# Softmax attention layer: TensorE's order over two positions, with three maxima in a row and one unit beside the values

## The reference, cut to what matters

```python
x = x + _layernorm(_L0_attn_ref(_layernorm(x), W_qkv, b_qkv, W_proj, b_proj))
# inside _L0_attn_ref
qkv = x @ W_qkv + b_qkv                       # split into q, k, v; 16 heads of 16
att = einsum('bhqd,bhkd->bhqk', q, k) * SCALE
att = where(causal, att, -inf); att = softmax(att, axis=-1)
y = einsum('bhqk,bhkd->bhqd', att, v)
return y.reshape(B, T, C) @ W_proj + b_proj
x = x + _layernorm(_L0_ffn_ref(_layernorm(x), weight, disha))     # same stage of the kernel
```

## Time and profile before

| what | value |
|---|---|
| median of 3 runs | 4210.25 us (4207.5 to 4215.37) |
| the profiled execution's own time | 4209.16 us |
| its span, first to last instruction | 4207.4 us |
| mean granted TensorE clock | 0.965 |
| softmax stage, first score matmul of batch 0 to the first of batch 7 | 103.6 to 1179.6 us |

### The profile page before, as it was taken

One profiled execution on the slowest core, in us unless ns is written; L12 is line 12 of the kernel. 1 busy time (PEld: TensorE's weight loads), 2 busy tenths in 40 slices (PEclk: granted clock), 3 DMA queues, 4 the chain that ended last, 5 costly groups with the idle time before them and its releaser, 6 DMA issues. The chain is left out here.

```text
span 4207.4 us, 74610 instructions
## 1 busy us (share of the span) xinstructions
PE 3893.2 (93%) x28676; PEld 3028.3 (72%) x28676; DVE 2712.3 (64%) x7778; ACT 2115.5 (50%) x3994; POOL 1172.9 (28%) x1083
## 2 busy tenths in 40 slices
PE   4999999999999899999999999999999599999993
PEld 2444444444545788888888888888888499999992
DVE  5888888888785565555565565555555555555555
ACT  1566666666666555554455554554454333333333
POOL 3233343343333211111112111111111133333335
PEclk8899999999988999999999999999999799999996
DMA  3543544443441100000000000000001133333345
GB/s 70 99 97 57 97 92 67 87 98 61 77 110 43 36 26 21 22 21 21 20 22 22 22 19 19 16 20 10 20 20 34 52 65 65 73 69 65 65 122 173
DMA packets 177203, 230.73 MB, mean 55 GB/s; under 512 B 27388, under 2 KB 152411, under 8 KB 176848
## 3 DMA queue, kind: packets, MB, share of 16 engines
q1 hardware_dynamic: 148816, 189.53, 19.6%
q0 software_dynamic: 25728, 28.03, 4.5%
q10 hardware_dynamic: 2304, 8.39, 0.5%
HBM read 94.30 MB, written 87.05 MB: 43 GB/s over the span
## 5 line engine op out<-in xcount | busy, mean ns | idle before, releaser
L880 ACT ACTIVATE probs<-a_scores 128x1024 f32<-128x1024 f32 (+3 forms) x768 | 615.7, 811 | 337.7 <-PE a_scores L774 331.8
L1034 DVE CUSTOM_DVE_ANT_0 a_scores<-a_scores,mask 128x384 f32<-128x384 f32 (+3 forms) x1024 | 480.6, 514 | 101.9 <-PE a_scores L760 96.2
L774 PEld LDWEIGHTS a_scores<-q_st,k_st 50*128 50x128 f32 x1536 | 149.1, 191 | 355.4 <-issue 201.5
L273 POOL TENSOR_TENSOR l_ln_rstd<-l_ln_ve,minus_half 128x4 f32<-128x4 f32 x80 | 82.0, 1025 | 1047.5 <-DVE l_ln_ve L246 1047.1
L1842 ACT ACTIVATE l_o<-l_num,l_den 128x64 f32<-128x64 f32 x960 | 222.0, 319 | 292.6 <-DVE l_den L2328 281.1
L774 PE MATMUL a_scores<-q_st,k_st 50*128 50x512 f32 (+3 forms) x1536 | 349.9, 453 | 10.3 <-DVE mx L1034 4.0
L760 PE MATMUL a_scores<-k_st,q_st 48*128 48x512 f32 (+3 forms) x1536 | 305.9, 396 | 50.7 <-ACT probs L880 22.1
L1037 DVE TENSOR_REDUCE mx<-a_scores 128x2 f32<-128x1024 f32 x256 | 309.9, 1221 | 60.8 <-PE a_scores L760 60.1
L794 PE MATMUL a_out<-probs,v_aug 128*32 128x512 f32 (+3 forms) x3072 | 345.1, 523 | 3.4 <-POOL probs L961 3.2
L961 POOL TENSOR_SCALAR_AFFINE_SELECT probs<-probs 128x512 f32<-128x512 f32 x256 | 164.8, 645 | 518.5 <-ACT probs L880 507.3
L2664 PE MATMUL e_out<-e_weights_hi,e_hT_hi 128*128 128x256 f32 x1088 | 303.8, 279 | 0.0
(11 more groups left out here) (294 smaller groups left out, 10569.4 us busy)
## 6 DMA issues: line engine op xcount, KB each, us to landing
q_st<-parts SPq DMA_DIRECT2D x192, 128.0 KB, 4.5
k_st<-parts SPq DMA_DIRECT2D x192, 128.0 KB, 6.8
expert_rows_scratch<-empty_row SPq DMA_DIRECT2D x34, 520.0 KB, 9.5
l_x<-x_scratch SPq DMA_DIRECT2D x32, 512.0 KB, 3.8
e_weights<-in_L_ffn_W_dram SPq DMA_DIRECT2D x16, 1024.0 KB, 7.3
e_rows<-expert_rows_scratch SPq DMA_DIRECT2D x24, 390.0 KB
e_rows<-expert_rows_scratch SPq DMA_DIRECT2D x16, 520.0 KB
x_in<-in_L_attn_x_dram SPq DMA_DIRECT2D x8, 1024.0 KB, 5.5
```

Of the source, the lines that this page charges most:

```text
L774: last = nc.tensor.matmul(psum_r[:, R.slot(u), h2, 0:w], k_st[rows, 2 * hg + pair, i * P:(i + 1) * P], q_st[rows, 2 * hg + pair, q0:q0 + w ...
L880: nc.scalar.activation(probs[:, k % 3, 2 * pair:2 * pair + 2, 0:w], psum_r[:, R.slot(u), :, 0:w], ACT.Exp).then_inc(R.evacuated[R.slot(u)], 1)
L1034: last = nc.vector.tensor_tensor_reduce(s, s, mask[:, HALF - w:HALF], 1.0, LEAST, ALU.add, ALU.max, out[:, h2, :])
```

## The change

TensorE takes positions in twos, k even. The order before, over two positions (S scores, M maxima, V values, U unit; the position, then the pair; L is k+16):

`S k,0 | M L,0 | V k-2 | S k,1 | M L,1 | U k | S k+1,0 | M L+1,0 | V k-1 | S k+1,1 | M L+1,1 | U k+1`

The order after:

`S k,0 | M L,0 | S k,1 | V k-2 | M L,1 | M L+1,0 | M L+1,1 | U k | V k-1 | S k+1,0 | S k+1,1 | U k+1`

`r_units` numbers the ring in that order. On VectorE, at odd positions, the reduction of pair 0 comes before the taking out of the unit, where it came after it. ScalarE's and GpSimd's orders stay. No instruction is added or taken away, and none changes its size.

```diff
     def r_units(u0, with_head):
         units = {}
-        for k in range(NK):
-            for pair in range(2):
-                units["S", k, pair] = u0 + len(units)
-                if k + LM < NK or with_head:
-                    units["M", k + LM, pair] = u0 + len(units)
+        for k in range(0, NK, 2):
+            more = k + LM < NK or with_head
+            units["S", k, 0] = u0 + len(units)
+            if more:
+                units["M", k + LM, 0] = u0 + len(units)
+            units["S", k, 1] = u0 + len(units)
+            if more:
+                units["M", k + LM, 1] = u0 + len(units)
+                units["M", k + 1 + LM, 0] = u0 + len(units)
+                units["M", k + 1 + LM, 1] = u0 + len(units)
+            units["S", k + 1, 0] = u0 + len(units)
+            units["S", k + 1, 1] = u0 + len(units)
         return units
...
         def turn(b, U, RU, with_head, with_tail, prepare=None):
-            for k in range(NK):
-                more = k + LM < NK or with_head
+            for k in range(0, NK, 2):
+                more, of = k + LM < NK or with_head, b + (k + LM) // NK
                 scores(b, RU, k, 0)
                 if more:
-                    maxima(b + (k + LM) // NK, b, RU, k + LM, 0)
+                    maxima(of, b, RU, k + LM, 0)
+                scores(b, RU, k, 1)
                 if k > 1:
                     values(b, RU, k - 2)
                 elif with_tail:
-                    values(b - 1, RU_TURN, NK - 2 + k)
-                scores(b, RU, k, 1)
+                    values(b - 1, RU_TURN, NK - 2)
                 if more:
-                    maxima(b + (k + LM) // NK, b, RU, k + LM, 1)
+                    maxima(of, b, RU, k + LM, 1)
+                    maxima(of, b, RU, k + 1 + LM, 0)
+                    maxima(of, b, RU, k + 1 + LM, 1)
                 if k in UNIT_AT and kept(UNIT_AT[k], with_head, with_tail):
                     unit(batch_of(b, UNIT_AT[k]), b, U, UNIT_AT[k])
+                if k > 1:
+                    values(b, RU, k - 1)
+                elif with_tail:
+                    values(b - 1, RU_TURN, NK - 1)
+                scores(b, RU, k + 1, 0)
+                scores(b, RU, k + 1, 1)
+                if k + 1 in UNIT_AT and kept(UNIT_AT[k + 1], with_head, with_tail):
+                    unit(batch_of(b, UNIT_AT[k + 1]), b, U, UNIT_AT[k + 1])
...
                 what = UNIT_AT.get(k - 1)
+                if k % 2 == 1 and more:
+                    reduce(b, b, RU, mk, 0)
                 if what and what[0] in ON_DVE and kept(what, with_head, with_tail):
                     of = (b - 1 if what[0] in TAIL_UNITS else
                           b + 1 if what[0] in HEAD_UNITS or what == ("N", 4) else b)
                     take(of, b, U, what)
-                if more:
+                if k % 2 == 0 and more:
                     reduce(b, b, RU, mk, 0)
```

## The result

The changed kernel takes 4327.05 us (median of 4 runs, 4323.68 to 4335.19) against 4208.88 of the kernel before on the same chip: ratio 1.0285, 95% interval 1.0271 to 1.030. The forecast was 4228, range 4170 to 4290. The sign was right and the size was not: 118 us slower instead of 18.

What follows compares the result with a forecast made beforehand. VectorE's chain of reductions (143.6 us a batch), plus 6.7 where TensorE binds, gave 150.3; waits made it 156.0 against 153.4. Over the whole kernel +18 on 4209.2 gave 4227, median 4228 us, range 4170 to 4290.

Steps and rivals of the forecast that it cites:

- the three waits on top: Per softmax batch, beyond 150.3: bank for units +2.8, ScalarE's bursts +2.6, late VectorE at k = 4 and 8 +0.3.
- ACT in bursts: ScalarE: four exps arrive close together, layer-norm applications between some, so exps and second maxima come late; +2.6 us a batch.
- Chain and PE alone: Softmax batch: VectorE's chain 143.6 us, plus 6.7 where TensorE's own time is longer, makes 150.3.
- the one bank: VectorE takes out an even position's unit behind two reductions, so the next unit on TensorE waits; +2.8 us a batch.
- number u waits for u-3: Ring rule: position k+2's pair 0 scores wait for the reduction of the third maxima in a row.
- The chain of three reductions: VectorE has three reductions before the next two positions may start; its chain alone takes 143.6 us a batch.
- DVE's idle time: Sign of being right: VectorE's idle time in a batch rises from 20.8 us to 23 or more, before L1034 and L1037.
- PE's busy time would fall by 5 or more: Sign of being right: TensorE's busy time per batch down by 5 us or more, with more idle before L774.
- The unit beside the values: TensorE, unit next to values on all 128 rows: saves 0.15 us per two positions, bounds 0 and 0.30.
- The merged group: TensorE: score pairs in three groups instead of four save about 0.15; a middle 512-column pair costs about 0.25 us.
- Rival 4: ScalarE and VectorE starve in turn, at k = 12 to 18 and 24 to 27: +54, 4280 us; chance 0.20.

Runs made afterwards that it cites:

- the fill: Changed kernel with matmuls repeated while TensorE would wait: in positions 0, 1, 12, 13, 4309.31 us; also in 14 to 17 and 44 to 47, 4303.13 us.
- the two kernels with short reductions: Every VectorE reduction reads only the first 64 columns of its maxima, without the mask: kernel before 4171.27 us, changed kernel 4202.54 us.
- the alternating order: Kernel before with TensorE in twos, score groups of three, scores and maxima alternating, VectorE's order as in the change: 4328.15 us; with ScalarE's order fitted too, 4289.58 us.

## Why the prediction was right and wrong

- **The step that failed: the three waits on top, put at +5.7 a batch, above all "ACT in bursts" at +2.6.** Chain and PE alone were to give 150.3. At full clock the batch takes 165.6 with the fill, some 164.5 without (estimate: less about 1), so what stands on top of them is about 14, not 5.7, if the 150.3 is right. That is some 8.5 of the 12.9 us by which a batch missed (168.9 against 156.0). The part on the one bank was about right (38 and 39: by the prediction's prices 5.3 for PE and 1.0 for the bank, 6.33 measured). What was too small is the waiting of the maxima for slots that ScalarE holds: 25.1 us a batch, where it was 9.9. The sum took PE's times for the long units without the ring's waits in front of them. Positions 36 and 37 show it: by the prediction's prices they come to 6.88, 7.72 measured, at clock 1.00.

```profile
907.22 0.64 PE L801 MATMUL a_out<-probs,v_aug 128*32 128x256 f32 x8
907.99 1.36 PE L767 MATMUL a_scores<-k_st,q_st 48*128 48x512 f32 x6
908.38 0.18 PEld L767 LDWEIGHTS a_scores<-k_st,q_st 48*128 48x128 f32 x2 [0.20 <-DVE mx L1054]
908.91 0.19 PEld L767 LDWEIGHTS a_scores<-k_st,q_st 48*128 48x128 f32 x2 [0.34 <-ACT probs L897]
909.28 1.99 PE L699 MATMUL a_general<-w_ffn,yT 128*128 128x256 f32 x8
911.21 0.42 PE L801 MATMUL a_out<-probs,v_aug 128*32 128x128 f32 x8
911.56 0.62 PE L781 MATMUL a_scores<-q_st,k_st 50*128 50x384 f32 x4
```

  The three maxima take 1.29 from their issue to that of the unit (907.99 to 909.28), where 0.8 was counted. By the ring's numbers the second of them waits for the first maxima's reduction and the third for the exp of the second scores, and the two rows of weight loads (908.38, 908.91) show just these: two waits that the prediction's list never had, as it went from "number u waits for u-3" straight to the longest one. In this pair bound by PE they add in full, 0.5; 0.2 more is the first exp's slot (maxima at 1.67, where PE's own times give 1.47), and 0.15 the saving at the unit that wasn't there.
- **The clock: a term that the sum did not have.** The prediction read 1.00 in the batch of before and took it as given. A change that makes PE wait in long pieces doesn't keep that: two falls in a batch, 1.7 and 2.2 us by the fill, are some 4 of the missed 12.9 us a batch, and the clock brought back was worth 24 of the 100 us in all. The prediction had even named 12 and 13 among its longest pairs. It also never priced a matmul at the low level, though the run of before holds such stretches (0.97 over batches 0 to 6).
- **The chain of three reductions: right where it binds, and sized within 0.25.** Positions 0 and 1: 6.0 forecast, 6.17 measured; second maxima at 1.62, measured 1.68. Positions 12 and 13: 7.8, measured 8.03. DVE's idle time was to rise to 23 or more; it is 36.6. The third maxima moved away gave 0.7 back in such a pair at full clock, and about half of the loss over 18 pairs. The sign that PE's busy time would fall by 5 or more didn't come: it rose from 145.6 to 151.7.
- **The unit beside the values mostly saves nothing: the 0.15 taken for it was wrong, its bound 0 was right.** In the rows above the F unit costs 1.93 in front of the values, as against 1.92 in front of scores, and the values behind it 0.35, as before. This is what the rule in the Trainium skill, TensorEngine Tiling (Array Packing), Tiling Modes, says of 128x128 and 128x32 as two modes: the trace agrees, and by that rule the prediction's sum would have been some 10 us higher. The exception agrees with it too: unit N runs on 128x32 like the values, and from its start to the scores behind the values 1.19 pass (810.21 to 811.40), where N and the values of 512 columns took 0.34 and 1.00 apart (N from 739.70 to 740.04 in batch 4 before). The merged group does save: the middle one of S M S costs 0.24 (906.65 to 906.89), forecast 0.25.

```profile
906.65 0.40 PE L767 MATMUL a_scores<-k_st,q_st 48*128 48x512 f32 x2
906.89 0.40 PE L781 MATMUL a_scores<-q_st,k_st 50*128 50x512 f32 x2
...
810.21 0.30 PE L740 MATMUL a_general<-ident,mx 128*32 128x128 f32 x1
810.22 0.63 PE L801 MATMUL a_out<-probs,v_aug 128*32 128x512 f32 x3
...
811.40 0.44 PE L781 MATMUL a_scores<-q_st,k_st 50*128 50x384 f32 x2
```

- **Rival 4 (ACT and DVE starve in turn, 4280) was the nearest**, and had 0.20. Of its two places, 12 to 18 grew and 24 to 27 did not (12.86 against 12.77). It too left the clock out; with two falls a batch it would have given some 4310 (estimate). The range's upper end was built from this rival alone, and so missed by 37 us.

The sign of the change was forecast for a reason that holds for most of the loss, the reductions; the size was not. What stays open: the 31 us between the two kernels with short reductions, and with it how much of the waits is ScalarE's. The rows point to its four exps in a burst and to slots given back late; no run made its work shorter in this order. And where exactly the clock falls after a wait wasn't settled: the fill in one place moved it to the next.

## What to carry to other kernels

A ring of few slots ties its two readers together: before the writer's order is changed, write down for every slot whom it now waits for, not only for the one that looks longest, and turn the queues of both readers with it (in the alternating order ScalarE's unturned queue alone cost 39 us). An engine that showed waits of 10% spread thin may carry them at no price, and pay for the same waits when they stand in one piece, as TensorE's granted clock can fall behind them. Compare variants position by position at equal clock first; the total mixes the waits with what the clock does behind them.

## What the runs showed of the hardware that had not been expected

- The granted clock of TensorE fell to about 0.6 over positions 2, 3 and 14, 15 behind pairs in which PE was busy 5.2 of 6.2 and 5.1 of 8.0 us; the values of 512 columns there took 1.87 (786.25 to 788.12) instead of 1.00, as the timeline of PE after shows. With 16 more matmuls in the waits of 12 and 13, positions 14 and 15 ran at 1.00.

```profile
786.25 1.93 PE L801 MATMUL a_out<-probs,v_aug 128*32 128x512 f32 x8
788.12 0.90 PE L767 MATMUL a_scores<-k_st,q_st 48*128 48x256 f32 x6
```

- The same program has such stretches in some batches and not in others (clock 0.94 and 0.99 in two batches of one run), which doesn't show in the totals: these agree within 0.4%.
- A change between the full array and its four column tiles costs no less than one to the row tiles (F unit 1.93 against 1.92). Cheaper were changes within the same tiling: 48 rows to 50 rows, 0.24 for 512 columns where 0.32 stands before another form, and unit N beside the values, both on the column tiles, 1.19 for the two against 1.34.
